# Eleven gate tiles rounded by GpSimd, one by VectorE and twelve by ScalarE, in the up-product stretch of the last FFN

## The chip, the core and the metric

One core of one Trainium2 chip runs the whole program. The time is the device time of one execution in microseconds. Engine names are those of the profile: PE (TensorE matmul), PEld (its weight loads), DVE (VectorE), ACT (ScalarE), POOL (GpSimd) and SP (SyncE, which only issues transfers here).

## What is computed

Two layers act on 4096 rows of 256: a linear cross-attention and a mixture of eight experts, then a softmax attention and a quantized FFN. The change lies in the FFN. Cut to what matters:

```python
def _L1_ffn_ref(x, w_gate, w_up, w_down):
    def act_qdq(x):
        qmax = 2.0 ** (ACT_BITS - 1) - 1.0
        scale = jnp.maximum(jnp.max(jnp.abs(x)) / qmax, 1e-12)
        return jnp.clip(jnp.round(x / scale), -qmax - 1.0, qmax) * scale

    def fixed_qdq_u16(x):
        scale = 1.0 / 65536.0
        return jnp.clip(jnp.round(x / scale), 0.0, 65535.0) * scale
    x = act_qdq(x)
    up = act_qdq(x @ lpbq_dequant(w_up).T)
    gate = act_qdq(x @ lpbq_dequant(w_gate).T)
    sig = fixed_qdq_u16(jax.nn.sigmoid(gate))
    gate = act_qdq(gate * sig)
    o = act_qdq(gate * up)
    return o @ lpbq_dequant(w_down).T
```

Each `act_qdq` needs the largest absolute value of a whole tensor before it can round an element of it. So the FFN falls into stretches with a barrier between them.

## The kernel before

The hidden width of 768 times 4096 rows is held as 24 tiles (`FT`) of 128 partitions by 1024 numbers. PE makes the 24 gate tiles first (`gslot`), and then the 24 up tiles (`uslot`). The stretch that matters here is the second one: PE makes the up tiles, and the other engines meanwhile turn the finished gate tiles into gate times sigmoid. There is no scheduler. The order on every engine is the order of the code, and semaphores with counts join the engines.

For gate tile n the steps are these:

- **Round:** `gq[n % 3]`, int16, from `gslot[n]` times the scale `qs[:, 5:6]`. VectorE does it for the seven n in `GATES_BY_DVE` (L1879, counted by `k_gd`), ScalarE for the other 17 (L2016, counted by `k_gq`).
- **Sigmoid:** ScalarE, from `gq[n % 3]` back into `gslot[n]` (L2024 for tiles that VectorE rounded, L2029 for its own; `k_sg`).
- **Round the sigmoid:** GpSimd, `sq[n % 3]`, uint16, from `gslot[n]` (L1770, `k_sq`).
- **Product:** VectorE, `gq` times `sq` into `gslot[n]`, with the maximum into `peak` (L1883, a custom instruction and a short read of its accumulator; `k_p`).

`gq` is a ring of three pieces of `wgateT`, and `sq` one of three pieces of `wupT`, so the profile names them by these. Beside these steps ScalarE copies up tile n + 1 out of its PSUM bank (L1990), and VectorE takes the largest absolute value of up tile n (L1834). The loop of GpSimd is the short one to know:

```python
for n in range(FT):
    pool.wait_ge(k_sg, n + 1)
    if n >= 1:
        pool.wait_ge(k_p, n)
    pool.tensor_scalar(sq[n % 3], gslot[n], 65536.0, 1.0, ALU.mult, ALU.mult).then_inc(k_sq, 1)
    if n % 3 == 0 and n // 3 + 2 < NS:
        rows_back(n // 3 + 2)
```

`k_p` counts finished products, so GpSimd starts on tile n only when the product of tile n - 1 is done. `rows_back(q)` (L1764) waits until PE is through with an input buffer and loads the next 1 MB of inputs into it for PE.

VectorE runs, for each n: the largest of up tile n, the rounding of gate tile n + 2 where it is its own, the product of tile n. ScalarE runs, for each n: the rounding of tile n + 1 where it is its own (a tile that it did not round gets its sigmoid ahead of that, one that it rounded behind it), and then the copy of up tile n + 1. A rounding of tile n waits for the product of tile n - 3, whose piece of the ring it takes.

After tile 23 the maxima are joined over the partitions (`spread(2)`: L1800, L2089, L1803, L2092) and the scales of the next stretch follow (L1903 to L1908). The next stretch starts from these scales on ScalarE, VectorE and GpSimd (L2050, L1917, L1779).

## Time and profile before

| | |
|---|---|
| three timed runs | 813.66, 817.49, 818.08 us |
| median | 817.49 us |
| span of the profiled execution | 814.1 us |
| up-product stretch in it, from the first gate rounding to the join of the maxima | 626.1 to 694.3 us |
| PE, DVE, ACT, POOL busy over the span | 85, 78, 60, 39% |

The profiled execution has no own time on the page besides its span, from its first instruction to its last. It lies 3.4 us below the median of the timed runs and 0.4 us above the lowest. In the timeline a row gives the start, the duration, the engine, the line, the operation with the tile written and the tiles read, and in brackets the idle time just before it with what ended it. Two instructions of one engine may overlap by some 0.1 us, since a duration includes the tail in which the next has begun. So the cost of an instruction in a queue is best read from start to start.

### The profile page before, as it was taken

What the parts mean: (1) busy time and instruction counts of PE and PEld (TensorE: products, weight loads), DVE (VectorE), ACT (ScalarE), POOL (GpSimd) and SP (SyncE); (2) the same over time, 40 slices, a digit from 0 to 9 for tenths busy, and PEclk for the clock granted to TensorE, in tenths of its full rate; (3) what the DMA queues carried; (4) which work ended last, traced back from release to release, by engine and by line L of the source; (5) the groups of instructions that cost most, each with busy time, mean ns of one, the idle gap of its engine ahead of it and who ended that gap; (6) DMA issues with size and microseconds to landing.
All of it is one profiled execution on the core that took longest, in us unless ns stands there. A gap on an engine that the chain in (4) does not pass through costs nothing.

```text
span 814.1 us, 11786 instructions
## 1 busy us (share of the span) xinstructions
PE 690.2 (85%) x4152; PEld 529.5 (65%) x4152; DVE 632.6 (78%) x1244; ACT 486.0 (60%) x621; POOL 313.7 (39%) x249
## 2 busy tenths in 40 slices
PE   6882029999999888999999999999999999009998
PEld 5761026899888754566566656577887888007998
DVE  5988894887777388887767675987888899997654
ACT  2223012554454437796896886666655999796873
POOL 4353604377677735234422420003440444693000
PEclk9995558999999999999999999999999999658999
DMA  9927523456644570010013000003310743201343
GB/s 299 339 81 257 200 80 110 127 137 146 178 88 58 108 254 1 1 47 27 1 47 130 1 27 27 27 27 133 127 52 1 261 152 131 76 0 53 125 135 104
DMA packets 59540, 84.95 MB, mean 104 GB/s; under 512 B 7904, under 2 KB 47712, under 8 KB 57952
## 3 DMA queue, kind: packets, MB, share of 16 engines
q1 hardware_dynamic: 49936, 61.09, 22.3%
q0 software_dynamic: 7872, 21.11, 10.5%
q10 hardware_dynamic: 1680, 2.08, 0.8%
q8 instruction: 30, 0.49, 0.3%
q14 instruction: 22, 0.18, 0.1%
HBM read 53.73 MB, written 30.54 MB: 104 GB/s over the span
## 4 chain that ended last, share of the span: by engine, by line
PE 63%; DVE 14%; ACT 7%; issue 4%; POOL 3%; DMA 1%; POOLq 0%; DVEq 0%; ACTq 0%
PE bank L2101 13%; PE bank L2363 11%; PE bank L2157 8%; PE bank L2387 5%; PE bank L1448 3%; PE bank L1482 3%; PE bank L1505 3%; PE bank L1542 3%; PE bank L1502 3%; DVE above L783 2%; PE bank L1463 2%; PE bank L1486 2%; ACT wgateT L2050 1%; DVE qx L1179 1%; ACT qT L1331 1%
## 5 line engine op out<-in xcount | busy, mean ns | idle before, releaser
L1305 ACT ACTIVATE x<-bank,bic 128x512 f32<-128x512 f32 x160 | 106.2, 697 | 34.1 <-PE bank L1482 32.6
L1179 DVE TENSOR_REDUCE qx<-bank 128x4 fp32r<-128x616 f32 x128 | 98.2, 796 | 27.0 <-PE bank L1448 25.6
L2101 PE MATMUL bank<-ux,uwh 128*128 128x512 f32 x384 | 96.6, 393 | 0.2 <-ACT ux L1995 0.2
L2101 PEld LDWEIGHTS bank<-ux,uwh 128*128 128x128 f32 x384 | 72.5, 189 | 16.0 <-issue 0.6
L1482 PE MATMUL bank<-qT,K 128*128 128x512 f32 x128 | 61.5, 490 | 3.5 <-ACT x L1305 2.0
L2324 ACT ACTIVATE wgateT<-bank 128x512 f32<-128x512 f32 x32 | 19.2, 599 | 65.7 <-PE bank L2363 65.7
L1448 PE MATMUL bank<-Kb,qTb 128*128 128x308 bf16 x256 | 53.2, 298 | 4.9 <-DVE qx L1179 2.2
L2101 PE MATMUL bank<-ux,uwl 128*128 128x512 f32 x192 | 52.0, 393 | 0.0
L1106 POOL CAST qx<-q 128x1024 fp32r<-128x1024 f32 x8 | 8.5, 1068 | 112.7 <-PE bank L1463 104.0
L2363 PE MATMUL bank<-xh,wh 128*128 128x512 f32 x128 | 50.0, 390 | 0.3 <-DVE xl L2297 0.3
L2363 PE MATMUL bank<-xl,wh 128*128 128x512 f32 x128 | 50.0, 390 | 0.0
L2363 PE MATMUL bank<-xh,wl 128*128 128x512 f32 x128 | 49.9, 390 | 0.0
L1448 PEld LDWEIGHTS bank<-Kb,qTb 128*128 128x128 bf16 x256 | 18.3, 97 | 46.3 <-DVE qx L1179 18.6
L2157 PE MATMUL bank<-uwh,oh 128*128 128x256 f32 x192 | 45.1, 277 | 0.5 <-DVE oh L1942 0.5
L2157 PE MATMUL bank<-uwl,oh 128*128 128x256 f32 x192 | 44.9, 276 | 0.0
L1331 ACT CAST qT<-bank 128x1024 fp32r<-128x1024 f32 x32 | 32.5, 1016 | 18.4 <-PE bank L1463 18.4
L2108 PE MATMUL bank<-uwh 128*128 128x512 f32 x39 | 12.0, 469 | 36.6 <-DVE peak L1834 36.6
L1121 POOL TENSOR_SCALAR q<-xr,mean,rstd 128x256 f32<-128x256 f32 x28 | 34.6, 1249 | 20.3 <-DVEq L1288 19.5
L2101 PEld LDWEIGHTS bank<-ux,uwl 128*128 128x128 f32 x192 | 36.6, 191 | 7.7
L707 POOL DMA_INDIRECT wupT<-row_dram,idx x16 | 16.5, 1030 | 56.7 <-DVE idx L869 28.0
L2157 PEld LDWEIGHTS bank<-uwh,oh 128*128 128x128 f32 x192 | 36.0, 188 | 1.0 <-DVE oh L1942 0.9
L2157 PEld LDWEIGHTS bank<-uwl,oh 128*128 128x128 f32 x192 | 36.1, 188 | 0.0
(420 smaller groups left out, 2029.0 us busy)
## 6 DMA issues: line engine op xcount, KB each, us to landing
xs_dram<-ux POOLq DMA_DIRECT2D x6, 1024.0 KB, 4.2
ux<-xs_dram POOLq DMA_DIRECT2D x6, 1024.0 KB, 5.3
x_dram<-x SPq DMA_DIRECT2D x4, 1024.0 KB, 5.5
xr<-in_w1T SPq DMA_DIRECT2D x8, 512.0 KB, 3.8
xr<-in_w3T SPq DMA_DIRECT2D x8, 512.0 KB, 4.7
xr<-in_w2T SPq DMA_DIRECT2D x8, 512.0 KB, 6.5
row_dram<-xn SPq DMA_DIRECT2D x8, 512.0 KB, 3.1
x_dram<-xr SPq DMA_DIRECT2D x8, 512.0 KB, 2.9
```

What stands on the lines that cost most here:

```text
L1121: pool.tensor_scalar(q[:, k, :, :], xr[:, t, :].rearrange("p (h d) -> p h d", d=HD), mean[:, t:t + 1], rstd[:, t:t + 1], ALU.subtract, ALU ...
L1179: dve.tensor_reduce(qx[:, k, g * GH:(g + 1) * GH, MROW].rearrange("p (u h) -> p u h", u=2), pair[i][:].rearrange("p (u x) -> p u x", u=2)[ ...
L1305: act.activation(pr[g % 2][h], S_[u % 2], ACT.Exp, bias=bic[:, s // 2, h // GH:h // GH + 1]).then_inc(p_done, 1)
L1331: act.copy(qT[s % 2][:, 2 * f:2 * f + 2, :, :].rearrange("p n k t -> p (n k t)"), pair[i][:]).then_inc(done[i], 1)
L1448: mm = pe.matmul(dst[:, u * QN:u * QN + 2 * S2], qTb[:, k, g, :], Kb[s // 2 % 2][:, g, u * 2:u * 2 + 2, :].rearrange("p h s -> p (h s)"), ...
L1482: mm = pe.matmul(dst, K[b % 2][:, at // 2, at % 2, :], qT[s % 2][:, at // 2, :, :].rearrange("p k t -> p (k t)"), start=True, stop=True)
L1502: pe.matmul(O_[n % 2][j * 32:(j + 1) * 32, :], V[b % 2][:, g * GH + j, :], pr[n % 2][j], start=True, stop=False, skip_group_check=True)
L1505: pe.matmul(O_[n % 2], Vr[b % 2][:, g, :], pr[n % 2][j], start=False, stop=True, skip_group_check=True).then_inc(v_done, 1)
L2101: mm = pe.matmul(bank[j][:, m * TB:(m + 1) * TB], w[:, c * HI + cols:c * HI + cols + P], x[:, part, c * TB:(c + 1) * TB], start=(w is uwh ...
L2157: mm = pe.matmul(bank[i % 2][:, k * D:(k + 1) * D], o[t % 3][:, m * TB + k * P:m * TB + (k + 1) * P], w[:, c * D:(c + 1) * D], start=(o is ...
L2363: mm = pe.matmul(bank[1 + m][:, (c % 2) * CAP:(c % 2 + 1) * CAP], wp[i][:, m, d * H + c * P:d * H + (c + 1) * P], xp[i][:, d, :], start=(n ...
L2387: mm = pe.matmul(bank[3][:, k * D:(k + 1) * D], hp[:, c, k * P:(k + 1) * P], wp[i][:, 2, c * D:(c + 1) * D], start=(c == 0 and n == 0 and ...
```

## The change

The rounding of gate tiles 3, 5, 7, ... 23 (eleven of them) is given to GpSimd, with a semaphore `k_gp` of its own. VectorE keeps tile 0, and ScalarE has 1, 2, 4, 6, ... 22 (twelve). In the loop of GpSimd the wait for the product of tile n - 1 now stands first, behind it the rounding of tile n + 2, and behind that the wait for the sigmoid of tile n and its rounding. ScalarE handles a tile of GpSimd as it did one of VectorE. The number of ScalarE's roundings enters a count of the next stretch (`gates_done`), which is adapted.

```diff
-            GATES_BY_DVE = (0, 4, 7, 10, 14, 17, 20)
+            GATES_BY_DVE = (0,)
+            GATES_BY_POOL = tuple(range(3, FT, 2))
+            GATES_BY_ACT = tuple(n for n in range(FT) if n not in GATES_BY_DVE + GATES_BY_POOL)
...
             def gates_done(i):
-                return FT - len(GATES_BY_DVE) + sum(k != POOL_AT[0] for k in range(i + 1))
+                return len(GATES_BY_ACT) + sum(k != POOL_AT[0] for k in range(i + 1))
...
                 for n in range(FT):
-                    pool.wait_ge(k_sg, n + 1)
                     if n >= 1:
                         pool.wait_ge(k_p, n)
+                    if n + 2 in GATES_BY_POOL:
+                        pool.tensor_scalar(gq[(n + 2) % 3], gslot[n + 2], qs[:, 5:6], 1.0, ALU.mult, ALU.mult).then_inc(k_gp, 1)
+                    pool.wait_ge(k_sg, n + 1)
                     pool.tensor_scalar(sq[n % 3], gslot[n], 65536.0, 1.0, ALU.mult, ALU.mult).then_inc(k_sq, 1)
...
                 def gate_integers(n):
-                    if n in GATES_BY_DVE:
+                    if n not in GATES_BY_ACT:
                         return
...
                     if n in GATES_BY_DVE:
                         act.wait_ge(k_gd, GATES_BY_DVE.index(n) + 1)
+                    if n in GATES_BY_POOL:
+                        act.wait_ge(k_gp, GATES_BY_POOL.index(n) + 1)
+                    if n not in GATES_BY_ACT:
                         act.activation(gslot[n], gq[n % 3], ACT.Sigmoid, scale=qs[:, 4:5]).then_inc(k_sg, 1)
                     if n + 1 < FT:
                         gate_integers(n + 1)
-                    if n not in GATES_BY_DVE:
-                        act.wait_ge(k_gq, sum(k not in GATES_BY_DVE for k in range(n + 1)))
+                    if n in GATES_BY_ACT:
+                        act.wait_ge(k_gq, GATES_BY_ACT.index(n) + 1)
                         act.activation(gslot[n], gq[n % 3], ACT.Sigmoid, scale=qs[:, 4:5]).then_inc(k_sg, 1)
```

GpSimd's queue before, at the start of the stretch (`wupT` is the ring of sigmoid integers, `ux` the input buffer of PE):

```order
L1770 TENSOR_SCALAR wupT<-low 128x1024 [waits k_sg]
L1764 DMA ux<-xs_dram 128x2048 [waits u_sent0,u_mm]
L1770 TENSOR_SCALAR wupT<-low 128x1024 [waits k_p,k_sg] x3
L1764 DMA ux<-xs_dram 128x2048 [waits u_sent1,u_mm]
L1770 TENSOR_SCALAR wupT<-low 128x1024 [waits k_p,k_sg] x2
```

The same place of GpSimd's queue now (`wgateT` is the ring of gate integers):

```order
L1774 TENSOR_SCALAR wupT<-low 128x1024 [waits k_sg]
L1766 DMA ux<-xs_dram 128x2048 [waits u_sent0,u_mm]
L1772 TENSOR_SCALAR wgateT<-low,qs 128x1024 [waits k_p]
L1774 TENSOR_SCALAR wupT<-low 128x1024 [waits k_sg]
L1774 TENSOR_SCALAR wupT<-low 128x1024 [waits k_sg,k_p]
L1772 TENSOR_SCALAR wgateT<-low,qs 128x1024 [waits k_p]
L1774 TENSOR_SCALAR wupT<-low 128x1024 [waits k_sg]
L1766 DMA ux<-xs_dram 128x2048 [waits u_sent1,u_mm]
L1774 TENSOR_SCALAR wupT<-low 128x1024 [waits k_sg,k_p]
```

At every second tile a gate rounding now stands ahead of the sigmoid rounding, and it is the gate rounding that waits for the product (`k_p`).

VectorE's queue before, at tiles 1 and 2 (`ISA` is the product and the read of its accumulator, `peak<-high` the largest of an up tile):

```order
L1834 TENSOR_REDUCE peak<-high 128x1 [waits u_f]
L1883 ISA low,peak<-wgateT,wupT 128x1024 [waits k_sq]
L1883 ISA peak 128x1
L1834 TENSOR_REDUCE peak<-high 128x1 [waits u_f]
L1879 TENSOR_SCALAR wgateT<-low,qs 128x1024 [waits k_p]
L1883 ISA low,peak<-wgateT,wupT 128x1024 [waits k_sq]
L1883 ISA peak 128x1
```

The same place of VectorE's queue now:

```order
L1838 TENSOR_REDUCE peak<-high 128x1 [waits u_f]
L1887 ISA low,peak<-wgateT,wupT 128x1024 [waits k_sq]
L1887 ISA peak 128x1
L1838 TENSOR_REDUCE peak<-high 128x1 [waits u_f]
L1887 ISA low,peak<-wgateT,wupT 128x1024 [waits k_sq]
L1887 ISA peak 128x1
```

The rounding of gate tile 4 is gone from between the largest of up tile 2 and the product of tile 2, and so are five more further on.

## Rows read from the trace of the kernel before

**Rows 1.** The page: its first line.
```profile
span 814.1 us, 11786 instructions
```

**Rows 2.** Windows: PE, PEld, DVE, ACT, POOL busy (instructions), PE clock, DMA share, GB/s.
```profile
640.00:650.00 10.00, 10.00 (x46) 8.29 (x45) 9.80 (x14) 10.00 (x11) 4.87 (x6) 1.00 0.82 263
...
670.00:680.00 10.00, 10.00 (x46) 8.29 (x45) 9.79 (x14) 9.91 (x11) 4.48 (x5) 1.00 0.29 107
```

**Rows 3.** Timeline, DVE: start, us, engine, line, operation, [idle before]; a plain tile.
```profile
683.14 1.23 DVE L1883 CUSTOM_DVE_ANT_0 high<-wgateT,wupT 128x1024 f32<-128x1024 int16 x1
...
684.29 1.21 DVE L1834 TENSOR_REDUCE peak<-low 128x1 f32<-128x1024 f32 x1
685.61 1.23 DVE L1883 CUSTOM_DVE_ANT_0 high<-wgateT,wupT 128x1024 f32<-128x1024 int16 x1
```

**Rows 4.** Timeline, POOL, between the two products of rows 3.
```profile
684.53 1.04 POOL L1770 TENSOR_SCALAR wupT<-high 128x1024 uint16<-128x1024 f32 x1 [1.42 <-DVE peak L1883]
```

**Rows 5.** Timeline, DVE, a tile with a gate rounding on VectorE.
```profile
677.48 1.23 DVE L1883 CUSTOM_DVE_ANT_0 high<-wgateT,wupT 128x1024 f32<-128x1024 int16 x1
...
678.63 1.22 DVE L1834 TENSOR_REDUCE peak<-low 128x1 f32<-128x1024 f32 x1
679.76 1.01 DVE L1879 TENSOR_SCALAR wgateT<-high,qs 128x1024 int16<-128x1024 f32 x1
680.70 1.21 DVE L1883 CUSTOM_DVE_ANT_0 high<-wgateT,wupT 128x1024 f32<-128x1024 int16 x1
```

**Rows 6.** Timeline, POOL and DVE, products of tiles 0 and 1.
```profile
629.22 1.23 DVE L1883 CUSTOM_DVE_ANT_0 low<-wgateT,wupT 128x1024 f32<-128x1024 int16 x1 [1.29 <-POOL wupT L1770]
...
632.48 0.58 POOL L1764 DMA_DIRECT2D ux<-xs_dram  x1 [3.29 <-PE bank L2101]
...
633.07 1.07 POOL L1770 TENSOR_SCALAR wupT<-low 128x1024 uint16<-128x1024 f32 x1
...
634.17 1.23 DVE L1883 CUSTOM_DVE_ANT_0 low<-wgateT,wupT 128x1024 f32<-128x1024 int16 x1 [2.42 <-POOL wupT L1770]
```

**Rows 7.** Timeline, all engines, end of the stretch.
```profile
686.88 1.15 ACT L2016 ACTIVATE wgateT<-high,qs 128x1024 int16<-128x1024 f32 x1 [0.27 <-DVE peak L1883]
...
689.13 3.73 PE L2140 MATMUL bank<-cst 128*128 128x128 f32 x32
...
690.02 1.46 ACT L2039 CAST uwh<-wdownT 128x1536 fp32r<-128x1536 f32 x1
...
693.01 1.23 DVE L1883 CUSTOM_DVE_ANT_0 high<-wgateT,wupT 128x1024 f32<-128x1024 int16 x1
...
694.28 0.20 DVE L1800 TENSOR_REDUCE amax<-peak 128x2 f32<-128x50 f32 x1
```

**Rows 8.** Line L1770, POOL's sigmoid roundings: ns min/median/max, first and last start.
```profile
L1770 POOL TENSOR_SCALAR wupT<-high x10: 1036/1043/1044, 668.5 to 691.9; 128x1024 uint16<-128x1024 f32 x10
```

**Rows 9.** Timeline, POOL, two roundings back to back after the stretch.
```profile
696.70 1.11 POOL L1779 TENSOR_SCALAR high<-high,qs 128x1024 int32<-128x1024 f32 x1 [3.72 <-DVE qs L1906]
...
697.80 1.11 POOL L1782 TENSOR_SCALAR high<-high,qs 128x1024 int32<-128x1024 f32 x1
```

**Rows 10.** Lines L1782 and L1121, other POOL instructions of this kind.
```profile
L1782 POOL TENSOR_SCALAR xnT<-xnT,qs x4: 1112/1122/1128, 711.5 to 737.0; 128x1024 int32<-128x1024 f32 x4
...
L1121 POOL TENSOR_SCALAR q<-xr,mean,rstd x28: 1208/1220/2031, 302.2 to 459.9; 128x256 f32<-128x256 f32 x28
```

**Rows 11.** Line L1879, VectorE's gate roundings, one of its forms.
```profile
L1879 DVE TENSOR_SCALAR wgateT<-high,qs x3: 798/1010/1218, 663.5 to 679.8; 128x1024 int16<-128x1024 f32 x3
```

**Rows 12.** Line L1764, the input loads of PE, and their time to landing.
```profile
L1764 POOL DMA_DIRECT2D ux<-xs_dram x6: 544/550/578, 632.5 to 673.3; - x6
...
DMA to landing us min/median/max: 5.0/5.3/6.8
```

**Rows 13.** Timeline, PE, the same place in two up tiles.
```profile
682.78 1.98 PE L2101 MATMUL bank<-ux,uwh 128*128 128x512 f32 x8
...
685.50 1.98 PE L2101 MATMUL bank<-ux,uwh 128*128 128x512 f32 x8
```

More of the change, by code:

```diff
@@ L1678, in build @@
             u_sent, u_back = ([sem(f"u_{n}{i}") for i in range(2)] for n in ("sent", "back"))
-            k_gq, k_gd, k_sg, k_sq, k_p, k_top, k_uq, k_du, k_p2, k_pg, k_om = (sem("k_" + n) for n in "gq gd sg sq p top uq du p2 pg om".split())
+            k_gq, k_gd, k_gp, k_sg, k_sq, k_p, k_top, k_uq, k_du, k_p2, k_pg, k_om = (sem("k_" + n) for n in "gq gd gp sg sq p top uq du p2 pg om".split())
             k_away, k_home = ([sem(f"k_{n}{i}") for i in range(2)] for n in ("away", "home"))
```

## The prediction

> **What bounds the kernel now.** I began with the page, for the span [rows 1], and with the list of lines, to find where the eleven, seven and 17 roundings lie: all between 626 and 694 us, one stretch, with a barrier at its end. Then I read the windows of that stretch [rows 2]. PE is busy all 10 of 10 us at full granted clock, ACT 10.0 and 9.9, DVE 9.8, POOL 4.9 and 4.5. Three engines look full and GpSimd half idle, and from these shares alone moving work to GpSimd looks like a gain. The question that the shares can't answer is who is last at the barrier, so I read the end of the stretch in the timeline [rows 7]. PE's last matmul of the up product ends where its next line begins, at about 689.1; ACT's last rounding is at 686.9, and at 690.0 it is already at work for the next stretch (the copy of the down weights). VectorE is last: the product of tile 23 starts at 693.01, and the join of the maxima at 694.28. PE is 4 us ahead of it. So the pace of the gate tiles decides, from product to product on VectorE, and PE's own pace of 2.72 us for a tile [rows 13] is a floor close behind.
>
> I then read that pace closely. Between two products without a gate rounding on VectorE [rows 3] it is 685.61 - 683.14 = 2.47 us, and two queues run side by side in it. VectorE does the product (1.15 from start to start) and the largest of an up tile, which ends at 685.50. GpSimd [rows 4] starts its sigmoid rounding at 684.53, that is 0.24 after the product ends its main part at 684.29, released by that product, takes 1.04, and VectorE starts 0.04 after it. So 2.47 = 1.39 (from the start of a product to the start of the next rounding) + 1.04 + 0.04. The idle 1.42 us ahead of the rounding is not free time of GpSimd in which it could do something for this chain: it is GpSimd waiting for the product. **The chain product, GpSimd, product is closed**, and whatever is put into GpSimd's part of it behind that wait lengthens it, unless VectorE has as much of its own to do.
>
> **What the change takes away.** Of VectorE's seven gate roundings tile 0's stays and six go. With one, a step takes 680.70 - 677.48 = 3.22 [rows 5], 0.75 above the plain one. All six together, with the small waits that the tiles have besides, I take from the whole stretch: from the product of tile 0 at 629.22 [rows 6] to that of tile 23 at 693.01 [rows 7] it is 63.79 us. The first step, from tile 0 to tile 1, is 4.95 [rows 6], since GpSimd's queue stands behind a wait for PE (the input load, issued at 632.48). The other 22 steps at the plain 2.47 would be 54.3. What is left, 63.79 - 4.95 - 54.3 = **4.5 us**, is all that relieving VectorE can give at that plain pace: 4.2 or so of it are the six roundings (six by about 0.7), the rest are waits of 0.1 to 0.2 for ScalarE and for PE ahead of an input load. I take the whole 4.5 as gained, since ScalarE has fewer roundings too. Even that much is above what PE leaves, as the first rival shows, but it is the right term as long as something slower takes its place.
>
> ScalarE loses five roundings of 1.15 [rows 7], which overlap by some 0.1. ScalarE was full, but it is not last at the barrier, and in the new order its sigmoid for a tile is done well before GpSimd asks for it. So I cost this at nothing: what hides it is the chain of VectorE and GpSimd, and if that chain were quick ScalarE would have needed the relief. The two new waits on ScalarE (for `k_gp`) stand ahead of the sigmoid and of the copy of an up tile. GpSimd rounds tile n two tiles ahead of its turn, so the sigmoid has a tile's time before it is needed.
>
> **What the change adds.** Eleven roundings on GpSimd, at n = 1, 3, ... 21, each behind the wait for the product of tile n - 1 and ahead of the sigmoid rounding of tile n, for which the next product waits. Each lies wholly in the closed chain, with only 0.1 us of cover: VectorE's own work in a plain step (the largest ends at 685.50, GpSimd's rounding at 685.57) has no more slack than that. The price of one: no row shows this very form (int16 out, float in, one scalar read from a tile, one constant). The nearest are the same instruction with int32 out, 1.11 long and 1.10 from start to start [rows 9], up to 1.13 in others [rows 10], and the same instruction with 16 bit out and two constants, 1.04 [rows 8]. These are my two ends, and I take 1.08 between them: the output is as narrow as in the one and the scalar as in the other. Eleven by 1.08 is **11.9 us**, by the ends 11.4 to 12.4. All of it lies on the path; the two roundings of a pair run on GpSimd one behind the other.
>
> The GPSIMD Engine Reference of the Trainium skill (elementwise, side-by-side cycle accounting, with the clock in its specifications) gives one-input work of at most two operations 1.03 cycles an element at 1.2 GHz. As an estimate from that page a rounding would be 0.88 us and eleven of them 9.7, with a sum of +5.2 where mine is +7.4. The start-to-start distance of 1.10 in this trace [rows 9] speaks for the dearer price, and I keep it.
>
> A new step with GpSimd's gate rounding is then 2.47 + 1.08 = 3.55, a plain one 2.47, a pair 6.02, which is 3.01 for a tile against PE's 2.72. The first step becomes 4.95 + 1.08 = 6.03, for the gate rounding stands behind the same input load. The products of tiles 1 and 23 fall at 629.22 + 6.03 = 635.25 and 635.25 + 10 by 3.55 + 12 by 2.47 = 700.39, and the second is 7.38 after the 693.01 of before. It agrees with 11.9 - 4.5 = **7.4 us later**.
>
> **What else moves.** The input loads of PE stand in GpSimd's queue behind the sigmoid roundings of tiles 0, 3, 6, 9, 12, 15. Before, each waited for PE [rows 12]. Now, with the gate chain slower than PE, the later ones are issued late. The last, behind tile 15, is issued at about 677.3 (product of tile 15 at 635.25 + 7 by 6.02 = 677.4) and lands 5.3 later, at 682.6; by PE's pace it is wanted three tiles before 689.2, at 681.1. So PE stalls by some 1.5 us, by 3 with the longest landing of 6.8 [rows 12], and ends at 691 to 692. That is still 8 us ahead of the last product, and the largest of up tiles 21 to 23 is asked for later than that. I cost it at nothing; its cover is the same lateness that causes it. The issue itself, 0.55 us, lies beside the product as before. ScalarE's copy of the down weights, at 690.0 for 1.5 us [rows 7], slips behind its last sigmoid, to about 695 to 697, and the scales of the next stretch come at about 704: hidden too. The next stretch begins from these scales with the same instructions and slips as a whole. On PE the small matmuls of the join come after a longer pause than before; I take them as equal.
>
> **The sum.** -4.5 + 11.9 = +7.4, with the ends of the price +6.9 to +7.9. The span becomes 814.1 + 7.4 = 821.5. The page gives no own time for the profiled execution besides the span, which is 3.4 below the median of the timed runs, so I add to the median: 817.49 + 7.4 = **824.9 us**, +0.9%.
>
> **The rivals.**
> (a) *The rounding fits into GpSimd's idle time.* Then VectorE and ScalarE are relieved and PE decides. The place is the wait at the head of GpSimd's loop: if roundings could run while the product of the tile before runs, each would have the 1.42 us of idle time, against a price of 1.08. PE ends at 689.1, and behind it VectorE has to do the largest of tile 23 (1.2) and the product (1.15), so the join is at about 691.6 instead of 694.3: -2.7, a time of 814.8. The decisive point is whether a rounding needs the product of tile n - 1; it waits for it by the code, as the order shows, and the idle time in the rows is put down to the product. Chance 4 in 100. Faster than this it can't be, by PE.
> (b) *The chain stretches by less than the rounding's length.* GpSimd would have to prepare the second of two instructions beside the first, and so pay some 0.7 to 0.95 for it. That is 7.7 to 10.5 - 4.5 = +3.2 to +6.0, 820.7 to 823.5. Against it: the pitch of 1.10 for two in a row [rows 9]. 13 in 100, and half of it is within 0.5%.
> (c) *The roundings are dearer than on the rows.* One row warns: a tensor_scalar with two scalars from tiles on only 256 columns takes 1.22 us [rows 10], almost five times the others per column. With 5 us each the time would be +50 us. The form of the change has one such scalar, like the rows at 1.11, so I give this extreme 2 in 100, and 8 to a milder one: 1.2 to 1.4 us each, or PE stalls that come back through ScalarE's queue, +8.7 to +11, 826 to 828.5.
> (d) *VectorE and GpSimd get in each other's way.* The trace shows such a thing: VectorE's own gate roundings, equal in shape, take from 0.80 to 1.22 us, the long ones beside a sigmoid rounding of GpSimd [rows 11]. Perfetto Trace Analysis of the Trainium skill (Optimizing Scalar/DVE Operations) says that the two engines share a read port, so that moving work from one to the other might not help. Here the wait for the product keeps the new rounding away from the only instruction that reads two tiles, and the largest, beside which it falls, is 1.21 next to a GpSimd rounding already [rows 3, 4]. So the port adds nothing to my sum; the same outcome comes from the queue. It is inside (c).
> That the change doesn't do what it says is excluded by the order.
>
> **The numbers.** The forecast has 73 in 100, (a) 4, (b) 13, (c) with (d) 10. A measurement of this kernel tells about 0.5%, 4.1 us, from no change. Slower by more than that: 73 + 10 + 6 = 0.87 with a little for scatter of the medians taken off; within it 0.10; faster 0.03. The three runs of before lie 4.4 apart, so the range is wider than the price alone: from 819.5, which takes in most of (b) and a low median, to 828.5, with the milder (c).
>
> **What would show it.** In the profile of the changed kernel: GpSimd's gate rounding at 1.04 to 1.12 us and the next sigmoid rounding directly behind it; VectorE idle for about 1.0 us ahead of every second product, released by GpSimd; steps of 3.55 and 2.47 in turn; VectorE's busy share in the stretch down from 9.8 to about 8 of 10, ScalarE's down too; the join of the maxima at about 701.7; short stalls of PE ahead of up tiles 18 and 21. I am wrong if the odd steps are below 3.2, if the pace is PE's 2.72, or if the stretch behind the barrier changes its length.

## The result

| | before | changed |
|---|---|---|
| median of the timed runs | 816.20 us (10 runs, 813.36 to 819.43) | 821.68 us (10 runs, 820.86 to 822.66) |
| ratio to before, 95% interval | | 1.0066 [1.0049, 1.0083] |
| span of the profiled execution | 814.1 us | 819.9 us |
| product of tile 0, start | 629.22 | 628.51 |
| product of tile 23, start | 693.01 | 698.27 |
| join of the maxima, start | 694.28 | 699.54 |
| from product 0 to product 23 | 63.79 | 69.76 |

The kernel became slower by 0.66%, 5.5 us between the medians, where 7.4 were forecast. The span grew by 5.8. The two profiles agree outside the stretch: up to product 0 the changed one is 0.7 us ahead, and from the second join, of the next stretch, to the end it is 72.2 us before and 72.3 after. So the difference is in the 24 tiles, and a little in the join itself and what follows it (47.6 us from this join to the second one before, 48.1 after).

Here are two windows of the changed kernel, columns as in [rows 2]:

```profile
650.00:660.00 10.00, 10.00 (x46) 8.29 (x45) 7.71 (x11) 8.32 (x9) 6.31 (x7) 1.00 0.43 122
...
690.00:702.00 12.00, 3.97 (x30) 3.19 (x28) 9.37 (x16) 3.67 (x4) 4.21 (x4) 0.75 0.26 87
```

From 650 to 660 VectorE is busy for 7.7 of 10 us, where the rows of before have 9.8, and ScalarE for 8.3 instead of 10.0. GpSimd is up from 4.5 or 4.9 to 6.3. No engine but PE is full any more, and yet the stretch is longer: nobody's busy time bounds it, the waits between two engines do. The timeline of VectorE at products 16, 17 and 18, to be held against [rows 3, 5] (L1887 is the product here, L1838 the largest of an up tile):

```profile
678.22 1.23 DVE L1887 CUSTOM_DVE_ANT_0 high<-wgateT,wupT 128x1024 f32<-128x1024 int16 x1
679.37 0.08 DVE L1887 DVE_READ_ACCUMULATOR2_ANT peak<- 128x1 f32 x1
679.37 1.21 DVE L1838 TENSOR_REDUCE peak<-low 128x1 f32<-128x1024 f32 x1
681.71 1.22 DVE L1887 CUSTOM_DVE_ANT_0 high<-wgateT,wupT 128x1024 f32<-128x1024 int16 x1 [1.13 <-POOL wupT L1774]
...
684.11 1.23 DVE L1887 CUSTOM_DVE_ANT_0 high<-wgateT,wupT 128x1024 f32<-128x1024 int16 x1
```

And GpSimd's beside it (L1772 is the gate rounding, L1774 the sigmoid rounding):

```profile
679.56 1.11 POOL L1772 TENSOR_SCALAR wgateT<-high,qs 128x1024 int16<-128x1024 f32 x1 [1.37 <-DVE peak L1887]
680.64 1.04 POOL L1774 TENSOR_SCALAR wupT<-high 128x1024 uint16<-128x1024 f32 x1
683.03 1.04 POOL L1774 TENSOR_SCALAR wupT<-high 128x1024 uint16<-128x1024 f32 x1 [1.35 <-DVE peak L1887]
```

The two roundings follow one another, 1.08 us from start to start, and VectorE stands idle for 1.13 until the second is done: 3.49 us from product to product. The next step has one rounding and is 2.40. From product 1 to product 22 the stretch repeats this pair. The list of line L1887 adds up VectorE's waits:

```profile
  POOL wupT L1774: 15.8, 12
```

Twelve waits, 15.8 us. One of 1.3 us ahead of product 0 was there before, and one of 3.5 ahead of product 1 was 2.4. The other ten are new, one of 0.8 and nine of 1.1. The end of the stretch, to compare with [rows 7]:

```profile
693.53 1.46 ACT L2046 CAST uwh<-wdownT 128x1536 fp32r<-128x1536 f32 x1
...
698.27 1.23 DVE L1887 CUSTOM_DVE_ANT_0 high<-wgateT,wupT 128x1024 f32<-128x1024 int16 x1
...
699.54 0.20 DVE L1804 TENSOR_REDUCE amax<-peak 128x2 f32<-128x50 f32 x1
...
699.80 0.58 PE L2096 MATMUL bank<-cst,amax 128*1 128x128 f32 x2 [7.00 <-DVE amax L1804]
```

ScalarE's copy of the down weights slipped by 3.5 us and is still far ahead of the join. PE has been idle for 7 us, and the two matmuls of the join take 0.58 us where they took 0.38.

### The profile page after: what moved, and what is told of

Read it like the earlier page. It is cut to its first block, busy times and chain, and to the rows that moved or that the text cites. A ratio compares the mean times of both kernels' runs of the same rounds, so it can differ in the third digit from the quotient of the medians.

```text
span 819.9 us, 11775 instructions
## 1 busy us (share of the span) xinstructions
PE 691.2 (84%) x4152; PEld 530.1 (65%) x4152; DVE 627.9 (77%) x1238; ACT 481.8 (59%) x616; POOL 325.7 (40%) x260
## 4 chain that ended last, share of the span: by engine, by line
PE 57%; DVE 15%; ACT 7%; POOL 6%; issue 5%; DMA 1%; POOLq 0%; DVEq 0%; SPq 0%; ACTq 0%
PE bank L2370 11%; PE bank L2108 8%; PE bank L2164 8%; PE bank L2394 5%; PE bank L1448 3%; PE bank L1482 3%; PE bank L1505 3%; PE bank L1542 3%; POOL wupT L1774 3%; PE bank L1502 3%; DVE above L783 2%; PE bank L1463 2%; PE bank L1486 2%; ACT wgateT L2057 1%; DVE qx L1179 1%
## 5 line engine op out<-in xcount | busy, mean ns | idle before, releaser
L1121 POOL TENSOR_SCALAR q<-xr,mean,rstd 128x256 f32<-128x256 f32 x28 | 34.6, 1249 | 20.3 <-DVEq L1288 19.5
```

The lines of the kernel that those rows point to most:

```text
L1121: pool.tensor_scalar(q[:, k, :, :], xr[:, t, :].rearrange("p (h d) -> p h d", d=HD), mean[:, t:t + 1], rstd[:, t:t + 1], ALU.subtract, ALU ...
```

## The experiments

Two theories stood at the start. **A, the closed chain:** product, GpSimd, next product; what GpSimd does between two products is paid in full. **B, the shared way into the memory:** VectorE and GpSimd slow each other, and the place in the queue matters little. In what follows the join is the start of the amax instruction, to be held against 694.28 before and 699.54 changed. It is read in profiles whose product 0 starts between 628.0 and 630.5, so differences below 1 us are read from product 0 on. Even that has a limit, which the run with six roundings shows: where PE stands at product 0 differs by 1.6 us from profile to profile, and this moves the first step. The two profiles of the result, before and changed, are alike in it.

### One wait order: the 0.07 us of a plain step

```diff
                 for n in range(FT):
-                    pool.wait_ge(k_sg, n + 1)
                     if n >= 1:
                         pool.wait_ge(k_p, n)
+                    pool.wait_ge(k_sg, n + 1)
```

> The kernel before, with only the two waits ahead of GpSimd's sigmoid rounding in the other order, that for the product first, as the changed kernel has them. Theory A (the order of the waits makes the wake-up quicker): a plain step from product to product goes from 2.47 to 2.40 us, the rounding starts 0.17 instead of 0.24 after the read of the accumulator begins, and the join of the maxima comes 0.9 to 1.5 us earlier than the 694.3 of before; the time within 0.2% of before. Rival B (plain steps are 2.40 in the changed kernel because VectorE and ScalarE have less to do): the steps stay 2.47 and the join stays.

Measured: 0.9999 [0.9981, 1.0017], join at 693.97, 63.62 us from product 0 to product 23. The plain steps are 2.38 to 2.40:

```profile
683.12 1.22 DVE L1883 CUSTOM_DVE_ANT_0 high<-wgateT,wupT 128x1024 f32<-128x1024 int16 x1
...
684.43 1.05 POOL L1770 TENSOR_SCALAR wupT<-high 128x1024 uint16<-128x1024 f32 x1 [1.35 <-DVE peak L1883]
...
685.51 1.22 DVE L1883 CUSTOM_DVE_ANT_0 high<-wgateT,wupT 128x1024 f32<-128x1024 int16 x1
```

So the first theory of this run's expectation, the quicker wake-up, holds for the step: with the wait for the product ahead of the other, GpSimd starts 0.16 us after the product's main part (684.27) and not 0.24. The changed kernel has the same order of waits, and its 2.40 needs no relief of VectorE to explain it. But the forecast of 0.9 to 1.5 us at the join failed; it came 0.3 earlier, 0.2 of it behind product 0. One place took 0.9 back. Behind the product of tile 2 VectorE has an instruction on one number for each partition (L1889). It took 0.16 us in the kernel before, and here:

```profile
638.82 1.05 POOL L1770 TENSOR_SCALAR wupT<-low 128x1024 uint16<-128x1024 f32 x1 [1.76 <-DVE peak L1883]
...
638.84 1.03 DVE L1889 TENSOR_TENSOR peak<-top_gq,top_sq 128x1 f32<-128x1 int16 x1
```

It now begins 0.02 us after GpSimd's rounding and lasts as long as that. Before, it began at 638.84, 0.06 ahead of the rounding at 638.90, and took 0.16.

### The rounding moved behind, beside the product

```diff
-                    if n + 2 in GATES_BY_POOL:
-                        pool.tensor_scalar(gq[(n + 2) % 3], ...).then_inc(k_gp, 1)
                     pool.wait_ge(k_sg, n + 1)
                     pool.tensor_scalar(sq[n % 3], ...).then_inc(k_sq, 1)
+                    if n + 2 in GATES_BY_POOL:
+                        pool.tensor_scalar(gq[(n + 2) % 3], ...).then_inc(k_gp, 1)
```

> The changed kernel, with GpSimd's gate rounding of tile n + 2 moved from ahead of the sigmoid rounding of tile n to behind it. It has the same work on every engine. Theory A (the rounding costs because it lies between a product and the next one; in the idle 1.36 us behind the sigmoid rounding it is free): the odd steps fall from 3.49 to about 2.4, GpSimd's idle time is used up, PE's 2.72 us a tile becomes the pace, and the join comes at about 692, 2.3 us before that of the kernel before and 7.5 before that of the changed one: ratio to before 0.997. Rival B (VectorE and GpSimd share a way into the memory): the rounding now falls beside the product, which reads two tiles; one of them gets longer by 0.5 to 1.1 us in every second step, and the join stays at 697 to 699.5, ratio 1.003 to 1.0066.

Measured: 1.0053 [1.0027, 1.0078], join at 697.10. GpSimd's gate roundings in this kernel (its L1774; ns min/median/max):

```profile
L1774 POOL TENSOR_SCALAR wgateT<-high,qs x5: 2179/2185/2186, 667.4 to 690.2; 128x1024 int16<-128x1024 f32 x5
```

and the product beside one of them:

```profile
679.07 2.18 POOL L1774 TENSOR_SCALAR wgateT<-high,qs 128x1024 int16<-128x1024 f32 x1
...
679.12 1.23 DVE L1887 CUSTOM_DVE_ANT_0 high<-wgateT,wupT 128x1024 f32<-128x1024 int16 x1
```

The rounding takes 2.18 us instead of 1.11, and the product 1.23 as ever; so it is in ten of the eleven. The rounding gets longer by 1.07, about what the product takes from its start to the start of the next (1.15): GpSimd makes almost no headway beside it and does its work afterwards, into the time in which it should have begun the next sigmoid rounding. The long steps are 3.17, 3.73 where a load for PE is issued as well. So B was right here, at the lower end of the join it named, and A's 692 was wrong. This is the rule of Perfetto Trace Analysis in the Trainium skill (Optimizing Scalar/DVE Operations), that the two engines share a read port and moving work between them might not help; the trace agrees, with 2.18 against 1.11. A plain idle time in GpSimd's row is thus not yet time in which it could work: here it could not while VectorE read two tiles.

### Six roundings, none and twice eleven: the price of one

```diff
-            GATES_BY_POOL = tuple(range(3, FT, 2))
+            GATES_BY_POOL = tuple(range(3, FT, 4))
```

> The changed kernel, with six tiles (3, 7, 11, 15, 19, 23) rounded by GpSimd, one by VectorE and 17 by ScalarE. Theory A (each GpSimd rounding adds its own length to the chain and nothing else does): five roundings fewer by 1.09 us, the join at 699.5 - 5.5 = 694.1, ratio to before 1.000. Rival B (the stretch is longer because the chain as a whole fell behind PE and ScalarE, not by the piece): the join stays at 697 or later. Rival C (ScalarE, back at 17 roundings without VectorE's seven, is the bound): steps without a GpSimd rounding are 2.7 instead of 2.4 and it is ScalarE that releases GpSimd.

Measured: 1.0020 [1.0002, 1.0039], join at 694.32. The steps give the price of one rounding: four of the five that lost theirs fell from 3.49 to 2.40, by 1.09, and those that kept it stayed at 3.49. So A holds for the step, and B and C fell as the main cause.

From product 0 to product 23 it is 64.30, against 69.76 with eleven. That this is 5.46 less, and five times 1.09 is 5.45, is luck, and so is the join within 0.2 us of A's. Four steps bring 4.4. The fifth, from product 2 to product 3, brings 0.1: VectorE's small instruction meets a rounding of GpSimd there, as in the first experiment, and takes 1.03. Three steps are 2.6, for GpSimd waits for ScalarE's sigmoid, a trace of C, and they give back 0.6. And the first step, which has its GpSimd rounding in both kernels, is 4.49 instead of 6.08. GpSimd's first load waits for PE: it is issued 3.3 us behind product 0 in the changed kernel and 1.7 behind it here, at 630.45. The cause is PE's clock at the start of the stretch: the first four matmuls of the up product take 2.05 us there and 1.19 here. The same window, first in the changed kernel and then in this run:

```profile
626.00:640.00 14.00, 14.00 (x60) 11.51 (x59) 8.66 (x13) 12.96 (x15) 6.47 (x7) 0.94 0.49 178
```
```profile
626.00:640.00 14.00, 14.00 (x64) 11.59 (x63) 10.52 (x14) 13.58 (x16) 6.41 (x7) 1.00 0.54 190
```

From 622 to 630 the granted clock was 0.79 on the mean in nine of the 13 profiles (before, changed, wait order, doubled, opened with the rounding behind, both with later loads, first step, and the one with 40 small matmuls) and 1.00 in four (rounding moved behind, six, the kernel before opened, roundings left out). In these four PE stands 1.6 us further ahead at product 0, and the first step is shorter by 0.7 to 1.6.

```diff
                     if n + 2 in GATES_BY_POOL:
+                        pool.tensor_scalar(gq[(n + 2) % 3], ...).then_inc(k_gp, 1)
+                        pool.wait_ge(k_gp, k + 1)
                         pool.tensor_scalar(gq[(n + 2) % 3], ...).then_inc(k_gp, 1)
```

> The changed kernel, with each of GpSimd's eleven gate roundings made twice, one behind the other, into the same place (with a wait of GpSimd on itself between them). Theory A (each rounding lies whole in the closed chain): the odd steps from 3.49 to about 4.65, 11 by 1.1 to 1.2 more, the join at 699.5 + 12.5 = 712, the span at about 832.5. Rival B (part of the rounding is covered by other waits): clearly less than 12 us more.

Measured: one run of 834.51 (the kernel before beside it had a median of 815.86), span 832.7, join at 712.62, 13.1 later than the changed kernel's. The odd steps are 4.72, which is 1.23 more: 1.08 for the rounding and 0.14 for its wait on the first.

```profile
681.82 1.12 POOL L1773 TENSOR_SCALAR wgateT<-high,qs 128x1024 int16<-128x1024 f32 x1 [1.37 <-DVE peak L1890]
683.04 1.12 POOL L1775 TENSOR_SCALAR wgateT<-high,qs 128x1024 int16<-128x1024 f32 x1
684.12 1.04 POOL L1777 TENSOR_SCALAR wupT<-high 128x1024 uint16<-128x1024 f32 x1
```

All ten later odd steps and the first one grew alike, 13.55 us from product 0 to product 23, so nothing of it was covered, as A says. It is one run and one profile. The loads for PE were late enough in this run to stop PE for 1.6, 3.0 and 3.1 us, and the join did not feel it.

```diff
-                    if n + 2 in GATES_BY_POOL:
-                        pool.tensor_scalar(gq[(n + 2) % 3], ...).then_inc(k_gp, 1)
...
-                    if n in GATES_BY_POOL:
-                        act.wait_ge(k_gp, GATES_BY_POOL.index(n) + 1)
```

> The changed kernel without GpSimd's eleven gate roundings and ScalarE's waits for them: gate tiles 3, 5, ... 23 take the integers that an earlier tile left in the ring, so the output is not the reference's. VectorE has one rounding, ScalarE twelve. It measures the relief alone. Theory A (PE is the floor behind the chain): the join at 691.7 to 692.5 where the chain alone, 22 steps of 2.40, would end at 687.5; so the six roundings taken from VectorE are worth 2 to 2.7 us at the join, not the 4.5 of the sum, ratio to before 0.997. Rival B (PE is no floor, or the sum is right): the join at 690 or earlier. Rival C (the relief gives nothing): 694.

This kernel leaves the eleven roundings out, so it is no version to use. Measured: 0.9983 [0.9965, 1.0001], join at 691.88. The steps are 2.40, but four are 3.4. One is the small instruction of the first experiment, which met a rounding again (L1891 here, 1.03 us). The three others are PE's pace, and it comes in through GpSimd's queue:

```profile
655.63 0.54 POOL L1766 DMA_DIRECT2D ux<-xs_dram  x1 [1.74 <-PE bank L2104]
656.21 1.05 POOL L1772 TENSOR_SCALAR wupT<-xr 128x1024 uint16<-128x1024 f32 x1
```

GpSimd waits 1.74 us for PE to be through with the buffer before it may issue the load, and the sigmoid rounding stands behind it. So the relief of VectorE and ScalarE, with the new order of the waits, gives 2.4 us at the join against the kernel before, 2.6 from product 0 on. That is too much, for this profile is one of the four with PE's full clock at the start, and GpSimd waits for PE at all six loads. PE ends its up tiles 58.4 us behind product 0 here and 59.9 in the kernel before. With PE as late as there, my estimate is 1.5 less: 1.1 us for the relief. The timed runs are faster by 0.17%, 1.4 us, and their interval holds both values and no change as well.

Giving the eleven roundings to GpSimd costs 8.6 us beside this run (71.0 against 62.4 from product 0 to the join), not 12.0. The run without them loses 2.9 in three steps to PE and 1.0 to the small instruction, which the changed kernel doesn't lose, and 0.2 to a wait for ScalarE; against that, its first step is shorter by 1.8 where a rounding is 1.1.

### The chain opened

```diff
                 for n in range(FT):
+                    if n >= 3:
+                        pool.wait_ge(k_p, n - 2)
                     pool.wait_ge(k_sg, n + 1)
-                    if n >= 1:
-                        pool.wait_ge(k_p, n)
```

> The kernel before, with GpSimd's sigmoid rounding of tile n waiting for the product of tile n - 3 (whose piece of the ring it takes) instead of n - 1. Theory A (the closed chain product, GpSimd, product is what bounds plain steps): the chain is open, plain steps fall to VectorE's own 2.28 or to PE's 2.72 where PE is behind, the join comes at about 691.6 to 692.5, ratio 0.997 to 0.998. Rival B (shared way into the memory): the rounding falls beside the product and slows it or itself, products of 1.23 us become 1.5 or more, and steps stay at 2.47 or grow, ratio 1.000 to 1.005.

Measured: 1.0000 [0.9977, 1.0022], join at 695.28 with product 0 late, at 630.47; 63.56 us from product 0 to product 23, 0.2 less than before, and the first step alone is 0.8 shorter, by PE's clock. The plain steps fall to 2.27, VectorE's own work. GpSimd's roundings, 1.04 until now, take 1.66 to 1.99 where they fall beside a product, and VectorE need not wait for them:

```profile
676.01 1.21 DVE L1883 CUSTOM_DVE_ANT_0 high<-wgateT,wupT 128x1024 f32<-128x1024 int16 x1
...
676.14 1.99 POOL L1770 TENSOR_SCALAR wupT<-high 128x1024 uint16<-128x1024 f32 x1 [0.29 <-ACT high L2024]
```

The gain is lost where VectorE gets longer. At the tiles with a rounding of its own this takes 1.2 us beside a rounding of GpSimd (1.19 at 672.62, where [rows 5] has 1.01), and the last two of these steps are 3.39 instead of 3.0 and 3.2. The small instruction takes 0.80. And where a rounding of GpSimd begins just ahead of a product, it is the product that gets longer; so the last step is 3.13 instead of 2.46:

```profile
690.90 2.06 DVE L1883 CUSTOM_DVE_ANT_0 high<-wgateT,wupT 128x1024 f32<-128x1024 int16 x1
```

Both theories were half right: the chain was what bounded plain steps, and once it is open the meetings of the two engines take its place.

The same opening in the changed kernel, with the gate rounding behind:

```diff
                 for n in range(FT):
-                    if n >= 1:
-                        pool.wait_ge(k_p, n)
-                    if n + 2 in GATES_BY_POOL:
-                        pool.tensor_scalar(gq[(n + 2) % 3], ...).then_inc(k_gp, 1)
+                    if n >= 3:
+                        pool.wait_ge(k_p, n - 2)
                     pool.wait_ge(k_sg, n + 1)
                     pool.tensor_scalar(sq[n % 3], ...).then_inc(k_sq, 1)
+                    if n + 2 in GATES_BY_POOL:
+                        pool.wait_ge(k_p, n)
+                        pool.tensor_scalar(gq[(n + 2) % 3], ...).then_inc(k_gp, 1)
```

> The changed kernel, with the sigmoid rounding of tile n ahead and waiting only for the product of tile n - 3, and the gate rounding of tile n + 2 behind it, waiting for the product of tile n - 1. Theory A (closed chain alone): the chain is open, the join comes at PE's pace, 692. Theory D (what the two last runs showed: a GpSimd rounding beside a product takes a product's length longer, 2.18 or 1.99 instead of 1.1): GpSimd needs, for two tiles, three roundings of 3.2 us and waits out two products of 1.06, 5.3 us or 2.66 a tile, about PE's 2.72; the join at 692 to 694 and GpSimd nearly always busy.

Measured: 1.0029 [1.0008, 1.0050], join at 695.90. The steps are 2.30 and 2.99 in turn, 2.65 on the mean of a pair, as the sum of three roundings and two products said. The join is later than the 692 to 694 that I gave, since the first steps are 5.0, 4.2 and 2.6 and PE's loads add 0.6 three times. From product 0 to product 23 it is 66.35, the shortest of the three orders with eleven roundings on GpSimd (66.90 moved behind, 69.76 changed), and still no better than the 63.79 of the kernel before.

### The first step, and a try at a faster kernel

Up to here the first step was 4.2 to 6.1 us in every profile but that of the doubled run (7.3). I took it for the wait of GpSimd's first load for PE and moved the loads by a tile, once with six roundings on GpSimd and once in the kernel before with its waits swapped:

```diff
-                    if n % 3 == 0 and n // 3 + 2 < NS:
+                    if n % 3 == 1 and n // 3 + 2 < NS:
```

> Six gate tiles rounded by GpSimd (3, 7, 11, 15, 19, 23), 17 by ScalarE, one by VectorE, and the input loads of PE issued behind the sigmoid roundings of tiles 1, 4, 7, 10, 13, 16 instead of 0, 3, 6, 9, 12, 15. Theory A (the first step of 4.5 to 6.1 us is GpSimd's wait for PE ahead of the first load, and the other steps sum to less than PE needs): the product of tile 1 comes at about 631.5 to 632 instead of 633 to 634.6, PE's pace decides, the join at 691.7 to 692.5, 2 us before the kernel before, ratio 0.997. Rival B (the later loads reach PE too late): PE stalls at up tiles 15 to 21 and the join stays at 693.5 or later, ratio 1.000 or above.

> The kernel before, with the two waits ahead of GpSimd's sigmoid rounding in the other order and PE's input loads issued one tile later. Theory A (the chain of VectorE and GpSimd was 4.9 us into the stretch when it began to run, and with 22 steps of 59 us left it ends at 694 for that reason): the product of tile 1 comes 2 us earlier and the join at 691.7 to 692.5, ratio 0.997. Rival B (up tiles arrive too late for VectorE's largest, or the loads too late for PE): the 2 us are given back in later steps, the join at 693.5 or later, ratio 0.999 to 1.000.

Measured: 1.0049 [1.0030, 1.0067] with the join at 696.14, and 1.0025 [1.0008, 1.0042] with the join at 694.74. Both expectations failed at their first point: the first step stayed 4.8. (Both profiles have PE's clock fallen at the start, as the kernel before has.) In the run with six:

```profile
632.93 1.04 POOL L1774 TENSOR_SCALAR wupT<-low 128x1024 uint16<-128x1024 f32 x1 [1.23 <-ACT low L2036]
```

It was ScalarE's sigmoid of tile 1 that was late, which stands behind the copy of up tile 1 (a wait for PE) and another rounding. The load had only hidden that; in the kernel before, the sigmoid ended 0.3 us ahead of the end of the load's issue. And the later loads did reach PE late (0.2 and 0.8 us of idle at 648.9). So I took both away:

```diff
-                    if n % 3 == 0 and n // 3 + 2 < NS:
+                    if (n == 1 or n and n % 3 == 0) and n // 3 + 2 < NS:
...
+                    if n == 0:
+                        act.wait_ge(k_gq, 1)
+                        act.activation(gslot[1], gq[1], ACT.Sigmoid, scale=qs[:, 4:5]).then_inc(k_sg, 1)
-                    if n in GATES_BY_ACT:
+                    if n in GATES_BY_ACT and n != 1:
```

> Six gate tiles rounded by GpSimd as in the run with six, and the two things taken away that hold the first step: GpSimd's first load for PE is issued behind the sigmoid rounding of tile 1 instead of tile 0 (the others where they were), and ScalarE does the sigmoid of tile 1 ahead of the copy of up tile 1, which waits for PE, instead of behind it. Theory A (the last two runs kept a first step of 4.8 us since ScalarE's sigmoid of tile 1 came at 631.6, behind that copy and a rounding): the product of tile 1 comes at 632 or earlier instead of 633.2 to 634.6, the chain catches up with PE, the join at 691.7 to 692.7, ratio 0.997. Rival B (up tiles that come at PE's pace hold the next steps): the gain of the first step is given back within five tiles, the join at 693.5 or later, ratio 0.999 to 1.002.

Measured: 1.0017 [1.0003, 1.0031], join at 695.58. The first step fell to 3.50, but the next ones were 3.05, 2.54, 4.03 and 3.50. By product 4 it had taken 13.1 us, as in the run with six and later loads, so the 1.2 us were gone: rival B. In the step of 4.03 GpSimd waits for PE, 2.44 us ahead of its second load at 640.76. ScalarE has 17 roundings here and, in this window, no idle time:

```profile
650.00:660.00 10.00, 10.00 (x45) 8.26 (x45) 8.61 (x11) 10.00 (x11) 5.43 (x6) 1.00 0.46 150
```

No complete version beat the kernel before. Of its 65.1 us from product 0 to the join VectorE is busy for 60.6 and ScalarE for 61.3, PE ends its up tiles after 59.9, and the closed chain links VectorE with GpSimd: little is left in any one of them.

### The matmuls of the join

```diff
-                for _ in range(16):
+                for _ in range(40):
                     pe.matmul(bank[3][:, 0:P], ident, ident, start=True, stop=True)
```

> The changed kernel, with 40 instead of 16 small matmuls that write nothing used, between the up product and the join, so that PE is at work until about 698.4. Theory A (the join's matmuls take 0.58 instead of 0.38 us a pair since PE had been idle for 7 us and its clock had fallen): they take 0.38 again, and from the join to the reciprocal it is 1.96 us as before instead of 2.37. Rival B (they are slow for another reason): they stay at 0.58. The span moves by at most 0.5 us.

Measured: the pair takes 0.38 us again, and from the join to the reciprocal it is 1.96 instead of 2.37:

```profile
701.34 0.38 PE L2096 MATMUL bank<-cst,amax 128*1 128x128 f32 x2 [1.55 <-DVE amax L1804]
```

A holds, in one profile. In the changed kernel PE's small matmuls end at 692.8. The granted clock is 1.00 until 694 and 0.50, the level of 1.2 GHz, from 696 on; the window 690 to 702 has 0.75 on the mean. With 40 small matmuls it is 1.00 from 696 to 704. The span, 821.0, says nothing on 0.4 us, since this profile reached product 0 1.5 us later than the changed kernel's. The steps of 3.49 and 2.40 are the same to the hundredth.

## Why the prediction came out as it did

**The direction, the mechanism and the range held.** The rounding of GpSimd stands whole in the closed chain, and single steps show it: 3.49 us with it, 2.40 where it was taken away, 4.72 where it was made twice (1.08 for the second one and 0.14 for its wait on the first). The steps alternate as said. VectorE's idle time, the falling shares of VectorE and ScalarE and the slipped copy of the down weights are as said.

**The price of a rounding.** 1.08 was taken, between 1.04 and 1.13. The instruction lasts 1.11 to 1.13, and from start to start it is 1.08. Ends and choice held; eleven of them are 12.0 instead of 11.9. The changed kernel's time of 821.7 lies in the range, and also in that of rival (b), 820.7 to 823.5: the time alone could not tell them apart, the steps do. Of the 3.2 us by which 824.9 was too high, 1.3 are the median of three runs from which I started, 817.49 where ten gave 816.20. The estimate from the GPSIMD Engine Reference of the Trainium skill, 0.88 and a sum of +5.2, came nearer to the measured total, but for another reason: the trace has 1.08 where that page makes 0.88.

**The term that was mis-sized is the plain step.** I carried the 2.47 us of a plain step over to the new kernel as if it were a property of the two engines. It held 0.07 us that hung on the order of two waits in GpSimd's code, and the change swaps them. The diff shows the swap, and I read it only as making room for the new rounding. Twenty-two steps by 0.07 are 1.5 us, and this is the difference between the 7.38 forecast from product 0 to product 23 and the 5.97 measured, but for 0.1. The swap alone, in the kernel before, brings the same 2.40. In the changed kernel it came without the loss at VectorE's small instruction: GpSimd's gate rounding, which now follows product 2, begins at 638.33, in the same hundredth as the small instruction, and that took 0.19. How near this is to 1.03 I had not seen.

**The relief of 4.5 us was right as book-keeping and would have been wrong as a promise.** As part of a sum in which something slower takes over, the 4.5 were gained in full. Taken alone it is worth 2.4 at the join by the profile that leaves the roundings out, and about 1.1 by the estimate for the same clock of PE. PE is the floor, as rival (a) had it, but by another way. I had counted the join 2.5 us behind PE's last up tile, at 689.1; it came 4.1 behind it, at 687.8, and what held the chain was GpSimd's wait for PE ahead of the loads. So it is luck that 691.9 stands where 691.6 was said.

**What moves with it.** I had PE stop by 1.5 us or so ahead of up tiles 18 and 21. It stopped once, for 0.31:

```profile
680.77 1.20 PE L2108 MATMUL bank<-ux,uwh 128*128 128x512 f32 x4 [0.31 <-DMA ux<-xs_dram]
```

The last load was issued at 675.73 and not at 677.3, since the steps were shorter. That it costs nothing was right, and the doubled run shows it for ten times as much. The join's own matmuls I had called equal; they cost 0.4 us with what follows them, and so one of my signs of being wrong, a change of length behind the barrier, came true in small. From product 0 to 23 +5.97, the head start of -0.71, the join +0.4 and 0.1 elsewhere make the 5.8 of the span.

**The rivals.** (a) fell, and more thoroughly than I had argued. I had said that roundings would fit into GpSimd's idle time if they didn't have to wait for the product. The rounding moved behind shows that they would not fit even so: beside the product a rounding took 2.18 instead of 1.11. (b) had a range of +3.2 to +6.0 with the measured total in it, but not its mechanism: the chain did stretch by the full 1.09. (c) did not come: the roundings took 1.11 to 1.13, and PE's one stop did not come back. (d) I had priced at nothing for this order, and rightly, for in it no rounding meets a product; the cost shows as soon as the order changes.

## What to carry to other kernels

When two engines hand a tile back and forth, the length of the loop is the sum of both parts and of the wake-ups, and neither engine looks full; moving work from the fuller to the emptier one lengthens the loop if it lands between the hand-overs. Before idle time of GpSimd is filled, look at what VectorE does in it: beside an instruction that reads two tiles, one of the two had to wait here. And a step that is carried over to a new kernel should be taken apart down to the waits ahead of it, for a change that only reorders two of them moves it. Where two profiles are compared, read the granted clock at the start of the stretch first: here it moved a step by up to 1.6 us, more than several of the edits did, and made one total agree by luck.

## What the runs showed of the hardware that I had not expected

- **A GpSimd rounding and an instruction of VectorE with two inputs did not run side by side: one waited out the other.** With the rounding moved behind, GpSimd's took 2.18 us instead of 1.11 and the product 1.23 as without it. In the opened kernel two products that began behind a rounding took 1.63 and 2.06 instead of 1.22 (at 641.44 and 690.90). An instruction of VectorE on one number for each partition, but with two inputs, took 1.03 instead of 0.16 in the six profiles in which it began 0.02 us after a rounding. Which of the two waits can't be told from the recorded starts: the roundings of 2.18 began 0.05 or 0.06 us ahead of the product and waited all the same, so this stays open. VectorE's own gate rounding, with one input tile, is longer too beside one of GpSimd ([rows 11] and 1.2 in the opened kernel); the largest of an up tile is 1.21 with and without.
- **PE's clock was kept in some profiles and lost in others after the same short pause.** In all 13 profiles PE rests for 1.3 and 0.5 us around the matmuls of the join ahead of this stretch. In nine of them the granted clock then fell, to 0.50 from 625 to 628 in the kernel before; in four it stayed 1.00. It set PE back by 1.6 us. What decides it stays open.
- **The order of two waits ahead of an instruction is worth 0.07 us** when the wait that is fulfilled last stands first in the code: GpSimd then starts 0.16 or 0.17 us behind the product instead of 0.24.
- **The last stretch of the kernel runs at two paces with the same granted clock.** Each is a profile's window of 10 us with PE full; first the kernel before, then the kernel before with later loads:

```profile
775.00:785.00 10.00, 10.00 (x91) 10.00 (x90) 5.21 (x6) 7.70 (x8) 0.00 (x0) 1.00 0.36 116
```
```profile
775.00:785.00 10.00, 10.00 (x87) 10.00 (x86) 6.10 (x5) 7.48 (x8) 0.00 (x0) 1.00 0.48 151
```

  There are 91 or 87 matmuls in 10 us, both at 1.00. From the second join to the end it is 72.2 to 72.8 us in the eight profiles with the quick pace and 74.5 to 76.0 in the five with the slow one, which are those of the rounding moved behind, of both opened chains, of the kernel before with later loads and of the omitted roundings. The edits don't touch that stretch. What selects the pace stays open; the traffic of the DMA queues does not, since the run with six has 151 GB/s in this window with 91 matmuls and that of the rounding moved behind 107 with 87. It is a likely part of the scatter of the kernel before, 813 to 820 us, and a reason why the small differences above are read from the steps and joins and not from the times.
